# Third attention layer: key and value projections of the context moved into the rounding stage and kept in DRAM

## What is computed

```python
q  = ln(fp8_linear(h, wq));   k  = ln(fp8_linear(h, wk));   v  = fp8_linear(h, wv)      # side 0
qx = ln(fp8_linear(h, wqx));  kx, vx = split(cond @ w_kv_x.T);  kx = ln(kx)              # side 1
o  = concat(gqa(q, k, v), gqa(qx, kx, vx));   x = x + fp8_linear(o / smooth, wproj)
```

## Time and profile before

| | |
|---|---|
| three runs | 1845.38, 1840.97, 1845.22 us (median 1845.22) |
| profiled execution | 1841.28 us, span of its trace 1839.5 us |
| rounding stage | 871 to 905 us of the span |
| main part | 905.8 to about 1313 us |
| one batch (two phases) in the steady part | 48.7 us |

### The profile page before, as it was taken

One profiled execution on the slowest core, in us unless ns is written; L12 is line 12 of the kernel. 1 busy time (PEld: TensorE's weight loads), 2 busy tenths in 40 slices (PEclk: granted clock), 3 DMA queues, 4 the chain that ended last, 5 costly groups with the idle time before them and its releaser, 6 DMA issues. The chain is left out here.

```text
span 1839.5 us, 25081 instructions
## 1 busy us (share of the span) xinstructions
PE 1526.5 (83%) x8600; PEld 980.9 (53%) x8600; DVE 1081.8 (59%) x2306; ACT 806.6 (44%) x1881; POOL 785.3 (43%) x954
## 2 busy tenths in 40 slices
PE   6566659999797799998399999999699989836772
PEld 5322225566465356565167777777555565525662
DVE  5999972222674644354768888888722254562336
ACT  2898963111333211112588888888521111412221
POOL 1277741000200289792177777777310000027772
PEclk9666558999698899999599999999899988858886
DMA  2298861110503111310200000000111100056656
GB/s 78 60 183 178 179 146 61 41 35 26 183 2 129 53 58 60 121 55 23 80 2 1 1 1 1 1 1 2 44 30 43 35 25 1 33 205 233 230 171 238
DMA packets 174223, 140.12 MB, mean 76 GB/s; under 512 B 141793, under 2 KB 154721, under 8 KB 170386
## 3 DMA queue, kind: packets, MB, share of 16 engines
q1 hardware_dynamic: 165314, 114.89, 21.8%
q0 software_dynamic: 6416, 22.03, 3.5%
q10 hardware_dynamic: 2368, 1.61, 0.3%
HBM read 85.43 MB, written 19.50 MB: 57 GB/s over the span
## 5 line engine op out<-in xcount | busy, mean ns | idle before, releaser
L1848 POOL CAST l0m_pi<-l0m_pf 128x1024 bf16<-128x1024 int16 x128 | 133.2, 1040 | 107.5 <-ACT l0m_pf L1915 105.7
L389 PE MATMUL l1e_gu<-x_normT,l1e_w 128*128 128x512 f32 x384 | 171.6, 601 | 0.0
L1451 PE MATMUL l2x_pr<-l_w,l2x_xq 128*128 128x512 bf16 x576 | 141.8, 385 | 35.5 <-ACT credits L42 35.5
L1915 ACT ACTIVATE l0m_pf<-l0m_s,l0m_bias,l0x_sq 128x1024 int16<-128x1024 f32 x128 | 153.9, 1205 | 17.8 <-DVE l0m_bias L1946 11.3
L1942 DVE TENSOR_REDUCE l0m_mx<-l0m_s 128x1 f32<-128x1024 f32 x128 | 155.6, 1216 | 4.8 <-PE l0m_s L1857 4.4
L1857 PE MATMUL l0m_s<-l0x_kT,l0x_qT 64*128 64x512 bf16 x256 | 69.7, 561 | 68.4 <-ACT l0m_pf L1915 65.6
L389 PE MATMUL l0e_gu<-x_normT,l0e_w 128*128 128x512 f32 x272 | 121.3, 600 | 0.0
L1578 DVE BATCH_NORM_STATS2 l2x_bn<-l2x_raw 128x6 f32<-128x128 f32 x384 | 83.3, 279 | 64.3 <-ACT l2x_raw L1519 64.3
L389 PEld LDWEIGHTS l1e_gu<-x_normT,l1e_w 128*128 128x128 f32 x384 | 74.0, 194 | 84.3 <-issue 83.2
L389 PE MATMUL l2e_gu<-x_normT,l2e_w 128*128 128x512 f32 x256 | 114.3, 601 | 0.0
L441 ACT ACTIVATE l1e_sil<-l1e_gu 128x512 f32<-128x512 f32 x48 | 28.6, 596 | 178.6 <-PE l1e_gu L389 178.6
(11 more groups left out here) (508 smaller groups left out, 3602.0 us busy)
## 6 DMA issues: line engine op xcount, KB each, us to landing
l3m_w<-in_l_moe SPq DMA_DIRECT2D x16, 1280.0 KB, 6.8
l1e_w<-in_l_ffn SPq DMA_DIRECT2D x24, 384.0 KB, 3.1
l_rows<-zero_row SPq DMA_DIRECT2D x8, 1024.0 KB, 11.1
l_w<-l_rows SPq DMA_DIRECT2D x8, 1024.0 KB, 11.8
l0e_w<-in_l_ffn SPq DMA_DIRECT2D x17, 384.0 KB, 3.0
l2e_w<-in_l_ffn SPq DMA_DIRECT2D x16, 384.0 KB, 3.0
ctx_tok<-l_route SPq DMA_DIRECT2D x8, 512.0 KB
l2q_wps<-in_l_wp SPq DMA_DIRECT2D x16, 256.0 KB, 2.7
```

Source lines behind the costliest of these rows:

```text
L389: last = nc.tensor.matmul(gu[half][:, m, :], w[:, c % SW, (2 * k + m) * P:(2 * k + m + 1) * P], pg.xnT[:, k, cols(n)], start=(k == 0), sto ...
L1451: last = nc.tensor.matmul(flat(pr[t % 2][:]), src[:, k, tokens], pg.l2_w3[:, part, k, at:at + W], start=(k == 0 and part == 0), stop=(k == ...
L1848: nc.gpsimd.tensor_copy(pi[:, n % 8, :], pf[:, n % 4, :]).then_inc(s["rounded"], 1)
L1915: nc.scalar.activation(pf[:, n % 4, :], s_ps[n % 3][:], ACT.Exp, scale=sq[:, b, h:h + 1], bias=bias[:, n % 4:n % 4 + 1], accum_out=sm[:, b ...
```

## The change

The context's 32 projections (8 batches, four pieces of 512 columns: two of keys, two of values) leave the main part. They run in the rounding stage instead: PE computes them into eight PSUM buffers `l2q_kv_ps`, ACT copies each to one of four SBUF buffers `l2q_kv`, and POOL's queue stores each (256 KB) to a scratch tensor `l2_kv` in DRAM. In the main part SP's queue fetches keys and values of a batch, up to two batches ahead, into `kx` and `vx`, which lie where the weights `l2_wx` were. DVE takes the statistics of the keys from `kx` and writes the normalised keys to `l2x_raw`; PE reads the values of side 1 from `vx`. In side 1 PE and ACT now do nothing for projections at t = 0, 1, 6 and 7.

```diff
+            @block.tensor
+            def _(pe):
+                for i in range(KV_STEPS):
+                    b, u = divmod(i, 4)
+                    if i >= 8:
+                        pe.wait_ge(kv_kept, i - 7)
+                    for k in range(KD):
+                        last = nc.tensor.matmul(kv_ps[i % 8][:], pg.ctxT[:, k, b * P:(b + 1) * P], pg.l2_wx[:, k, u * W:(u + 1) * W],
+                                                start=(k == 0), stop=(k == KD - 1))
+                    last.then_inc(kv_done, 1)
+
+            @block.gpsimd
+            def _(pool):
+                for i in range(KV_STEPS):
+                    pool.wait_ge(kv_kept, i + 1)
+                    pool.dma_start(pg.l2_kv[i], kv[:, i % 4]).then_inc(kv_stored[i % 4], 16)
...
+                def keep_kv(i):
+                    act.wait_ge(kv_done, i + 1)
+                    if i >= 4:
+                        act.wait_ge(kv_stored[i % 4], 16 * (i // 4))
+                    nc.scalar.activation(kv[:, i % 4], kv_ps[i % 8][:], ACT.Copy).then_inc(kv_kept, 1)
...
                     for q in range(2 * n - 2, 2 * n):
                         if q >= 0:
                             keep(q)
+                            keep_kv(q)
                 keep(14)
                 keep(15)
+                for i in range(14, KV_STEPS):
+                    keep_kv(i)
...
+            @block.sync
+            def _(sp):
+                for b in range(B):
+                    for i in range(4):
+                        sp.wait_ge(kv_stored[i], 16 * (b + 1))
+                    if b >= 2:
+                        sp.wait_ge(s["normed"], item((b - 2, 1)) * 6 + 2)
+                    for u in range(2):
+                        sp.dma_start(kx[:, b % 2, u], pg.l2_kv[4 * b + u].rearrange("p (j d) -> p j d", j=U)).then_inc(kx_in[b % 2], 16)
+                    if b >= 2:
+                        sp.wait_ge(s["valued"], item((b - 2, 1)) * 4 + 4)
+                    for u in range(2):
+                        sp.dma_start(vx[:, b % 2, u * W:(u + 1) * W], pg.l2_kv[4 * b + 2 + u]).then_inc(vx_in[b % 2], 16)
...
-                        if pi is not None and t < 8:
+                        if projects(pi, t):
...
-                                for k in range(KD):
-                                    last = nc.tensor.matmul(flat(pr[t % 2][:]), pg.ctxT[:, k, tokens], pg.l2_wx[:, k, at:at + W],
-                                                            start=(k == 0), stop=(k == KD - 1))
...
+                            if projects(pi, t):
+                                dve.wait_ge(s["raw"], projected(pi, t) + 3)
+                                rows = raw[:, t]
+                            else:
+                                dve.wait_ge(kx_in[pi[0] % 2], 16 * 2 * (pi[0] // 2 + 1))
+                                rows = kx[:, pi[0] % 2, t]
```

More of the change, by code:

```diff
@@ L1283, in attention_l2 @@
         wp_in = [pg.sem(f"l2q_wp_in{i}") for i in range(4)]
+        kv_done, kv_kept = pg.sem("l2q_kv_done"), pg.sem("l2q_kv_kept")
+        kv_stored = [pg.sem(f"l2q_kv_stored{i}") for i in range(4)]
+        KV_STEPS = 4 * B
         with ExitStack() as st:
@@ L1292, in attention_l2 @@
             wps = sb("wps", [P, 4, 2, D])
+            kv = sb("kv", [P, 4, W])
+            kv_ps = [st.enter_context(nc.psum_tensor(f"l2q_kv_ps{i}", [P, W], F32)) for i in range(8)]
             block = st.enter_context(nc.Block())
@@ L1341, in attention_l2 @@
                  "recip", "p_normed", "p_turned", "p_kept", "valued", "o_read", "qsteps2", "widened", "quanted", "y_done", "y_added", "aff_in", "aggr", "y_scale", "smooth")
+        kx_in, vx_in = ([pg.sem(f"l2x_{m}_in{i}") for i in range(2)] for m in ("kx", "vx"))
         s = {m: pg.sem(f"l2x_{m}") for m in names}
@@ L1400, in item, with projected, projects, values @@
                 return pair[0] * 2 + pair[1]
+            def projected(it, t):
+                return it[0] * 12 + (t if it[1] == 0 else 6 + t)
+            def projects(it, t):
+                return it is not None and (it[1] == 0 or 2 <= t < 6)
+            def values(it):
+                return vx[:, it[0] % 2] if it[1] else pg.xnT[:, 0]
+            @block.sync
[11 more added lines that the diff above has]
+                        sp.dma_start(vx[:, b % 2, u * W:(u + 1) * W], pg.l2_kv[4 * b + 2 + u]).then_inc(vx_in[b % 2], 16)
             @block.gpsimd
@@ L1441, in fn @@
                     for t in range(8):
[L1442 removed]
+                        if projects(pi, t):
                             side = pi[1]
[L1444 removed]
+                            pe.wait_ge(s["raw"], projected(pi, t) + 1)
                             tokens = slice(pi[0] * P, (pi[0] + 1) * P)
[L1446 to L1457 removed]
+                            src = xq[:, (K_, K_, Q_, Q_, Q_, Q_, V_, V_)[t] if side == 0 else QX]
+                            at = t * W if side == 0 else 4096 + (t - 2) * W
+                            for k in range(KD):
+                                for part in range(3):
+                                    last = nc.tensor.matmul(flat(pr[t % 2][:]), src[:, k, tokens], pg.l2_w3[:, part, k, at:at + W],
+                                                            start=(k == 0 and part == 0), stop=(k == KD - 1 and part == 2))
                             last.then_inc(s["proj"], 1)
```

33 lines of the change are left out of this document (19 added, 14 removed).

## The result

The changed kernel is slower: 1861.06 us median (1857.96 to 1862.42, 4 runs) against 1843.53 us (1840.97 to 1845.38, 4 runs) for the kernel before, a ratio of 1.0086 with a 95% interval of 1.0069 to 1.0104. Forecast was 1827.5 us in a range of 1809 to 1840, so sign and size were both missed. The profiled execution took 1861.6 us, its span is 1859.9.

The account below looks back on a forecast made before the run. PE was taken to bound the main part at 48.7 us a batch. Terms -37 + 22.8 - 1.4 = -15.6 us took the profiled 1841.3 to 1825.7; set against the median too, the prediction was 1827.5, range 1809 to 1840.

Parts of the forecast that it names:

- What it is worth there: Main part: removing context projections saves 2.3 us a pair, giving a batch of 44.1 us; -37 us, ends -29 and -43.
- a sign of being wrong: Main part: the forecast is wrong if PE waits for DVE's or POOL's results rather than for ACT; no size given.
- DVE takes over: Main part: more than half of DVE's waits stay, batch 45.1 to 46 us, total -7 to 0, 1834 to 1845; chance 0.17.
- The rounding stage: Stage before the main part: 55.0 us of PE work, 34 us covered, main part begins 22.8 us later; bounds 22 and 28.
- the ring of four: Rounding stage's four SBUF store buffers: copy, issue and landing need 1.1 us a step, under PE's 1.72, so no cost.
- The rival of slow stores: Rounding stage paced by stores: gain gone at a 9.1 us trip; with 12.7 us landing, 52 us longer, 1878; chance 0.07.
- The rule that spoke for it: Rounding stage: GpSimd writing DMA descriptors is locked out of a shared port during VectorE's two-port modes; no separate size.
- POOL's issue of the last store: Rounding stage's end, behind PE's last projection: POOL takes 0.96 us to issue the final store.
- The clock at the main part's start: Main part's first 5.6 us: slow clock costs 2.8 us now; even odds that it stays up, half taken: -1.4 us.
- Nothing is late, cost zero: Main part: SP's fetches of keys and values arrive before they are wanted, so they add no time.

Follow-up runs that it names:

- The experiment with the earlier scaling: Changed kernel, but in side 1 DVE scales both key rows at t = 3 and 4 instead of 4 and 5: 1852.41 us, ratio 1.0092.
- the first four kernels: Kernels compared with 1837.58 us before: old kernel plus rounding work alone; changed kernel without later fetches, with eight extra matmuls, with earlier key scaling; ratios 1.0199, 1.0130, 1.0075, 1.0092.
- the second four: Changed kernel with earlier key scaling and lighter POOL, stores on SP, four batches precomputed, four with earlier scaling; against 1845.24 us before, ratios 1.0018, 1.0038, 0.9979, 0.9978.
- the last three: Changed kernel with extra matmuls and four batches precomputed, five batches, or all eight with stores on SP; against 1838.84 us before, ratios 0.9992, 0.9995, 1.0041.

## Why the prediction was wrong

The forecast of the profiled execution was off by 36 us (-15.6 against +20.4), 25 of them in the main part, 3 in the rounding stage, 8 outside of both.

**The step that failed is "What it is worth there":** "I take the middle of 1.8 and 2.7, since both engines are close and neither is tied to PE in every step: 2.3 a pair, a batch of 44.1 us". DVE is tied to PE, in just one step, and a batch takes 47.5. What I had named as a sign of being wrong, PE waiting for DVE and not for ACT, is what the profile shows. The two pairs of a batch are not alike. The one at t = 0, 1 of side 1 went from 6.95 to 5.19 us (rows of PE below) and saved 1.8. The one at t = 6, 7 went from 6.95 to 7.08, and the slow clock reaches 0.4 us into the pair behind it (6.52 from projection to projection instead of 6.09). That is 1.8 - 0.1 - 0.4, by the exact figures 1.2 us a batch.

```profile
1084.73 1.06 PE L1516 MATMUL l2x_s<-l2x_kT,l2x_qT 128*128 128x128 f32 x8
...
1089.92 1.46 PE L1508 MATMUL l2x_pr<-l_w,l2x_xq 128*128 128x512 bf16 x5
```

The row that said so was on my page: this pair holds 6.75 us of DVE work in 6.95. I wrote it down, and went on that DVE "catches up in the other", as if its work could be spread over the batch. It can't be: DVE's order is fixed, its list in this pair begins with statistics of a projection that PE has just made, and PE wants the list's result at the pair's end. A mean over the batch (41.5 us held of 41.8) was the wrong question. What counts is the way from PE's projection through ACT and DVE back to PE, 9.2 us, against the 7.25 us that PE has left to do. The experiment with the earlier scaling shows it: with the list in another order this wait is gone.

**The rival "DVE takes over"** named the right engine, with a batch of 45.1 to 46 us and a total of -7 to 0. It lacked two things. One is the granted clock: I counted PE's waits at their own length, and a wait of 2.0 us brings the clock down for 3.6 us behind it, seven times in eight here, 1.5 us a batch by the experiment with extra matmuls. The Trainium skill ("TensorE: Matmul & The Clock Gate", section "Why this matters for your kernels") warns of gaps between bursts of matmuls in the middle of a kernel, and here one of 2.0 us, shorter than those it speaks of, was enough; I thought of the clock for the main part's start only, not for the waits that the change itself makes. The other is that the chains are several: behind DVE stands POOL, behind POOL stands ACT. With DVE's wait and the clock behind it taken out, and then most of POOL's, a batch went from 47.5 to 46.5 and 45.2 us; the 44.1 of the forecast was not reached by any kernel here.

**The rounding stage** was right in mechanism and size: +25.5 for +22.8. Full clock from its start, ACT's jobs and DVE's chain undisturbed (DVE 36.38 us busy, before 36.36), no wait in the ring of four. The rival of slow stores fell: 0.54 us of issue and 2.3 us to landing (the longest 5.1), so a step of the ring needs (0.6 + 0.54 + 2.3) / 4 = 0.86 us, half of PE's 1.72. The rule that spoke for it (the Trainium skill, "SBUF — State Buffer", section "SBUF: two separate sides") doesn't bite in this stage: 15 stores were issued while DVE was busy 28.8 of 34 us, and the longest of all 32 took 0.67. Which of DVE's instructions here run in such a mode, no run shows. The missing 2.7 us are in POOL's wait for its queue at the end (3.4 us, shown by moving the stores), less what I had put too high in POOL's issue of the last store (0.96 for 0.54).

**The clock at the main part's start** (-1.4): wrong. It fell in the 5 us of the stage's end and the main part started at 1.2 GHz as before. With the stores on SP's queue PE stood for only 1.7 us and the granted clock stayed at 1.00 (930 to 940 us), yet the main part lasted the same 395.5. The timeline shows where the gain went: PE's first scores began 17.5 us behind PE's start in both kernels. With the clock up PE was 1.6 us ahead until its two first short waits (1.11 us for DVE and 0.96 for ACT, in both kernels), and there, at 946.84, the clock fell in this kernel and not in the changed one. So this term was worth nothing in either case.

**"Nothing is late, cost zero"** for the fetches: right, by the run without them.

**Outside of both stages** I counted zero. The profiled execution has 8 us there. What the two stages don't explain is from -2 to +12 us in the twelve comparisons (each ratio times the median of before, less the change of the two windows), and positive in eleven. They go with the group: 7 to 12 in the first four kernels, 4 and less in the second four and in the changed kernel itself, 5 to 9 in the last three. The windows of before are those of one profile, of none of these groups, so a part of this is the reference and not the change. The profiles show the granted clock of later stages falling at other moments, but one execution of each kernel is profiled and the first layer differs as well, so what share the change causes stays open.

## What to carry to other kernels

Work moved under another engine's cover is free up to the cover's end and costs its full length beyond it, so size the part that is moved by the cover, less what must still follow its last step: half of this change gained 0.2% (and with extra matmuls, in another comparison, nothing that can be told) where all of it lost. When work is taken out of the engine that bounds a loop, look at each stretch for the longest way that starts at this engine and comes back to it, with the fixed order of the engines in between, and not at the totals of the loop. A wait newly made on TensorE has to be priced with the clock that may fall behind it.

## What was unexpected of the hardware

- A wait of 2.0 us inside a part in which PE otherwise works without a gap can be enough for the granted clock to fall, and it stays at 1.2 GHz for 3.6 us of dense work. It fell behind seven of the eight waits of the changed kernel, six of eight with the stores on SP's queue and two of four with four batches. Eight matmuls without use in place of each wait shorten the main part by 6.0 us of 395.4.
- The rounding stage with its last DMA on POOL's queue ended 3.4 us later than with its last DMA on SP's (4.79 and 1.34 us from the last copy to the main part). In both kernels SP waits for the stores' semaphores before it fetches, so nothing relies on the longer wait.
- Two DVE instructions beside which POOL runs one of 512 columns take 1.01 and 1.08 us, where the same ones take 0.29 and 0.68 elsewhere, before the change as after it. They are 1.1 us of the chain that PE waits for.
- The fourth layer's attention, the same instructions in every kernel here, takes 93.4 to 100.5 us by its profiled executions, with a mean granted clock of 0.91 to 0.83.
